# A four-layer fp32 transformer block on one core: gating of the first chunk a step earlier, normalising in halves, maxima searched one slot sooner, opening statistics spread

## The reference, cut to what matters

```python
x = x + attention_a(layernorm(x))   # 16 heads of 8, q and k RMS-normed per head, softmax, projection
x = x + feed_forward(layernorm(x))
x = x + attention_b(layernorm(x))   # differential attention: rope, 16 score heads of 8, 8 value heads of 16
x = x + feed_forward(layernorm(x))

def feed_forward(xt):               # the same weights both times
    scores = softmax(xt @ gate_w.T)             # 8 experts
    top_scores, sel = top_k(scores, 2)
    for e in range(8):                          # routed input is xt times the expert's score
        h = silu(xe @ w1[e]) * (xe @ w3[e]);  out += h @ w2[e]
    out += (silu(xt @ w1s) * (xt @ w3s)) @ w2s  # shared expert
```

## Time and profile before

| | |
|---|---|
| median of 3 runs | 957.07 us (956.77 to 957.42) |
| the profiled execution's own time | 963.01 us |
| its span, first to last instruction | 961.2 us |
| PE busy | 846.6 us (88%) |
| DVE busy | 708.4 us (74%) |
| ACT busy | 557.1 us (58%) |
| POOL busy | 575.8 us (60%) |
| mean granted clock of TensorE | 0.934 |

### The profile page before, as it was taken

How to read it: one execution, slowest core, us unless ns; L and a number is a source line. 1 busy time by engine, 2 the same in 40 slices (tenths; PEclk the granted TensorE clock), 3 DMA queues, 4 the chain that set the end, 5 groups by cost and what they waited for, 6 DMA issues and landing times.

```text
span 961.2 us, 21825 instructions
## 1 busy us (share of the span) xinstructions
PE 846.6 (88%) x6976; PEld 596.9 (62%) x6976; DVE 708.4 (74%) x1916; ACT 557.1 (58%) x888; POOL 575.8 (60%) x666
## 2 busy tenths in 40 slices
PE   3789999988988988899788888888888899898998
PEld 2455555555777777787555555555544587777786
DVE  7777777784677776776668898989865587677674
ACT  1578788875533333344378888888864444444343
POOL 4766666681666556665427676767632776566662
PEclk9999999997899999999689999999975799999999
DMA  7000000000222222221000000000000223333331
GB/s 204 17 2 1 0 0 0 1 2 15 83 80 89 89 78 77 77 89 34 1 2 3 2 1 1 1 1 1 2 2 3 88 89 100 89 100 93 94 101 44
DMA packets 35695, 42.25 MB, mean 44 GB/s; under 512 B 5936, under 2 KB 18992, under 8 KB 35632
## 3 DMA queue, kind: packets, MB, share of 16 engines
q1 hardware_dynamic: 34048, 40.85, 13.7%
q10 hardware_dynamic: 1584, 0.62, 0.2%
HBM read 38.83 MB, written 2.36 MB: 43 GB/s over the span
## 4 chain that ended last, share of the span: by engine, by line
PE 32%; POOL 25%; DVE 19%; issue 18%; DMA 3%; ACT 2%; POOLq 0%; DVEq 0%; ACTq 0%
POOL f_xe_lo L1457 8%; POOL f_p L1469 7%; DVE s_mxs L1135 6%; PE psum L392 5%; PE psum L855 3%; POOL s_inv L1089 3%; PE psum L1372 3%; PE psum L823 3%; PE psum L362 3%; PE psum L423 2%; DVE s_qt L703 2%; DMA f_gt<-gates 2%; DVE f_xe L1493 2%; PE psum L1334 2%; PE psum L378 2%
## 5 line engine op out<-in xcount | busy, mean ns | idle before, releaser
L1457 POOL TENSOR_TENSOR f_xe_lo<-f_xe,f_xe_hi 128x512 fp32r<-128x512 f32 x96 | 123.2, 1289 | 146.0 <-ACT f_xe_hi L1431 146.0
L1431 ACT ACTIVATE f_xe_hi<-f_xe 128x512 fp32r<-128x512 f32 x128 | 80.8, 631 | 222.3 <-DVE f_xe L1493 222.3
L1135 DVE TENSOR_REDUCE s_mxs<-psum 128x4 fp32r<-128x1024 f32 x128 | 155.8, 1219 | 32.4 <-PE psum L840 31.1
L1509 DVE TENSOR_TENSOR f_h<-psum,f_g 128x512 f32<-128x512 f32 x144 | 99.1, 688 | 100.4 <-PE psum L1336 55.2
L1372 PEld LDWEIGHTS psum<-w,f_h 128*128 128x128 f32 x1152 | 152.4, 197 | 17.4 <-DVE f_h L1509 7.7
L1372 PE MATMUL psum<-w,f_h 128*128 128x128 f32 x1152 | 159.4, 283 | 2.6 <-DVE f_h L1509 2.5
L996 ACT ACTIVATE s_probs<-psum 128x1024 f32<-128x1024 f32 x128 | 131.2, 1025 | 45.0 <-PE psum L823 43.1
L493 ACT ACTIVATE s_probs<-psum 128x1024 f32<-128x1024 f32 x128 | 126.2, 1023 | 32.8 <-PE psum L378 32.3
L1334 PE MATMUL psum<-f_xe_hi,w_hi 128*128 128x512 f32 x288 | 132.2, 459 | 8.6 <-POOL f_xe_lo L1457 8.6
L1335 PE MATMUL psum<-f_xe_hi,w_lo 128*128 128x512 f32 x288 | 118.1, 410 | 0.0
L1336 PE MATMUL psum<-f_xe_lo,w_hi 128*128 128x512 f32 x288 | 116.1, 403 | 0.0
(11 more groups left out here) (178 smaller groups left out, 1568.0 us busy)
## 6 DMA issues: line engine op xcount, KB each, us to landing
f_gt<-gates SPq DMA_DIRECT2D x128, 256.0 KB, 3.3
x<-in_x SPq DMA_DIRECT2D x8, 256.0 KB, 6.0
out<-x SPq DMA_DIRECT2D x8, 256.0 KB, 4.7
w<-in_w SPq DMA_DIRECT2D x3, 512.0 KB, 5.8
s_qt<-s_mt SPq DMA_DIRECT2D x32, 8.0 KB
rope_cos<-in_rope_cos SPq DMA_DIRECT2D x1, 256.0 KB, 3.3
rope_sin<-in_rope_sin SPq DMA_DIRECT2D x1, 256.0 KB, 3.1
gates<-f_sg SPq DMA_DIRECT2D x16, 16.0 KB
```

The lines of the kernel that those rows point to most:

```text
L1135: dve.tensor_reduce(mxs[:, km % 2, p, r:r + 2, :, c:c + 1].bitcast(F32R), room(km, i).rearrange("p (r j s) -> p r j s", r=2, j=2), AX.X, A ...
L1457: pool.tensor_tensor(xe_lo[:, ring(e), :], src, xe_hi[:, ring(e), :], ALU.subtract).then_inc(xe_lo_pool.sem, 1)
```

## The change

1. `STATISTICS`/`ROOTS`: parts 2 to 7 of the opening's statistics move from steps -1, 0 and 1 to one part at position 12 of each of the steps 0 to 5, their roots to position 14. `normalise` of attention a waits by a new table `NORMED`.
2. The attention steps written out singly in a go up to 5 (`PEELED_A` = 6), so the loop has three turns of two steps; in b it stays (`PEELED_B` = 2).
3. `LEAD`: positions e = 0 to 4 of the feed-forward's step -1 move from step 15 into step 14 of both attentions, e = 5 to 7 are placed at h = 7, 10, 13 of step 15.
4. `FF`: `normalise` is split into tiles 0, 1 at e = 3 and tiles 2, 3 at e = 4; `best` goes from e = 7 to 6, `index` from 8 to 7, `residual` from 3 to 4, `moments` from 6 to 7, and the root of f's statistics from e = 8 to e = 1 of the next step.
5. On PE, `x_turn` is issued after `down(e)` instead of before it.

```diff
-STATISTICS = {(-3, 0): (0,), (-3, 12): (1,), (-1, 8): (2,), (-1, 12): (3,), (0, 4): (4,), (0, 11): (5,), (1, 4): (6,), (1, 9): (7,)}
-ROOTS = {(-3, 0): (0,), (-2, 5): (1,), (-1, 13): (2, 3), (0, 14): (4, 5), (1, 14): (6, 7)}
+STATISTICS = {(-3, 0): (0,), (-3, 12): (1,), (0, 12): (2,), (1, 12): (3,), (2, 12): (4,), (3, 12): (5,), (4, 12): (6,), (5, 12): (7,)}
+ROOTS = {(-3, 0): (0,), (-2, 5): (1,), (0, 14): (2,), (1, 14): (3,), (2, 14): (4,), (3, 14): (5,), (4, 14): (6,), (5, 14): (7,)}
+NORMED = {0: 1, 2: 2, 4: 3, 6: 4, 8: 5, 9: len(PARTS)}
+PEELED_A, PEELED_B = 6, 2
...
-LEAD = {0: (0,), 2: (1,), 3: (2,), 5: (3,), 6: (4,), 12: (5,), 13: (6,), 15: (7,)}
+LEAD = {(NSEQ - 2, 5): (0,), (NSEQ - 2, 7): (1,), (NSEQ - 2, 9): (2,), (NSEQ - 2, 11): (3,), (NSEQ - 2, 13): (4,),
+        (NSEQ - 1, 7): (5,), (NSEQ - 1, 10): (6,), (NSEQ - 1, 13): (7,)}
...
 FF = {
-    "norm": 4, "x_turn": 5, "xt_sb": 5, "logits": 6, "best": 7, "pow": 7, "index": 8, "masks": 0, "sums": 1, "gates": 2,
-    "residual": 3, "stats": 5, "moments": 6, "rstd": 8, "shared": 4,
+    "norm": (3, 4), "x_turn": 5, "xt_sb": 5, "logits": 6, "best": 6, "pow": 7, "index": 7, "masks": 0, "sums": 1, "gates": 2,
+    "residual": 4, "stats": 5, "moments": 7, "rstd": 1, "shared": 4,
 }
...
-                for m, km in turned(n, k, e, "x_turn"):
-                    x_turn(m, km)
                 for m, km in turned(n, k, e, "logits"):
                     logits(m, km)
                 if run:
                     down(e)
+                for m, km in turned(n, k, e, "x_turn"):
+                    x_turn(m, km)
...
-                if first and 0 <= k - 1 < NCH and e == FF["rstd"]:
+                if first and 0 <= k - 2 < NCH and e == FF["rstd"]:
+                    pool.wait_ge(vare_sb.sem, vare_sb.upto(n - 2))
+                    pool.tensor_tensor(
+                        rstd_next[:, :].rearrange("p (n c) -> p n c", c=4)[:, (n - 2).at, :], g.f_vare[:],
+                        g.minus_half[:, 0:4], ALU.pow).then_inc(rstd_sb.sem, 1)
+
+                if first and k == NCH and e == E:
                     pool.wait_ge(vare_sb.sem, vare_sb.upto(n - 1))
...
-                if k + 2 < NCH and e == FF["norm"]:
-                    normalise(n + 2)
+                if k + 2 < NCH and e in FF["norm"]:
+                    normalise(n + 2, (0, 1) if e == FF["norm"][0] else (2, 3))
...
-    with eng.Fori(0, 5) as i:
-        body(Step(i, 2, 2), 2)
-        body(Step(i, 2, 3), 3)
-    for n in range(12, NSEQ - 1):
+    with eng.Fori(0, (12 - peeled) // 2) as i:
+        body(Step(i, 2, peeled), peeled)
+        body(Step(i, 2, peeled + 1), peeled + 1)
+    for n in range(12, NSEQ - 2):
         body(Step(None, 0, n), n)
-    for h in range(HEADS):
-        body(Step(None, 0, NSEQ - 1), NSEQ - 1, (h,))
-        for e in LEAD.get(h, ()):
-            following(Step(None, 0, -1), -1, (e,))
+    for n in range(NSEQ - 2, NSEQ):
+        for h in range(HEADS):
+            body(Step(None, 0, n), n, (h,))
+            for e in LEAD.get((n, h), ()):
+                following(Step(None, 0, -1), -1, (e,))
```

More of the change, by code:

```diff
@@ L582, in normalise @@
             def normalise(m, km):
-                if km in (0, 2, 4, 6):
-                    dve.wait_ge(g.normed, {0: 1, 2: 2, 4: 3, 6: len(PARTS)}[km])
+                if km in NORMED:
+                    dve.wait_ge(g.normed, NORMED[km])
                 dve.wait_ge(xt_mm.sem, xt_mm.upto(m - 2))
@@ L1509, in hidden, with normalise @@
                 dve.tensor_tensor(g.f_h[:, q, :], H3[q], g.f_g[:, q, :], ALU.mult).then_inc(h_sb.sem, 1)
-            def normalise(m):
+            def normalise(m, half=range(4)):
                 if k == -1:
@@ L1519, in normalise @@
                 dve.wait_ge(xt_mm.sem, xt_mm.upto(m - 1))
-                for c in range(4):
+                for c in half:
                     dve.tensor_scalar(
@@ L1662, in feed_forward, with attention_steps @@
     return layer
-def attention_steps(eng, body, first, following, tail, opening=None, preceding=None):
-    for n in range(first, 2):
+def attention_steps(eng, body, first, peeled, following, tail, opening=None, preceding=None):
+    for n in range(first, peeled):
         for h in range(HEADS):
@@ L1708, in all_steps @@
 def all_steps(eng, o, a, f, b, h):
-    attention_steps(eng, a, -3, f, TAIL_A, o)
+    attention_steps(eng, a, -3, PEELED_A, f, TAIL_A, o)
     feed_forward_steps(eng, f, b)
-    attention_steps(eng, b, -1, h, TAIL_B, None, f)
+    attention_steps(eng, b, -1, PEELED_B, h, TAIL_B, None, f)
     feed_forward_steps(eng, h)
```

## The result

The changed kernel took 936.79 us (median of 4 runs, 934.12 to 938.77), the kernel before, on the same chip, 957.25 (956.77 to 959.90). The ratio is 0.9769, 95% interval 0.9742 to 0.9797: 2.3% faster. The forecast was 921.6, the range 905 to 938. The sign was right and the time is at the slow edge of the range: 20.5 won instead of 35.5. The profiled execution took 938.77 (span 936.9), 24.3 less in span than the profiled one of before.

A forecast was written before the change was run, and what follows sets the result against it. PE, busy 88%, was held in the feed-forwards by waits and low clock. Feed-forward 23.3 + opening 4.4 + leads 5.5 and 3.0 − root 0.7 = 35.5, taken off the median 957.07: 921.6, range 905 to 938.

The forecast's parts named there:

- Rivals 1: Feed-forward: PE's new wait for `xt_sb` before `logits` drops the clock, 1.3 a step; time 934; chance 0.17.
- 2: Feed-forward: PE is the bound, the halves of `normalise` hide entirely; periods 22.4, time 902; chance 0.13.
- 4: Feed-forward: `best` is late, `pow` starts no sooner, `low(4)` stays late; f gains 1.2 a step, time 934; chance 0.05.
- the ring: Feed-forward: the cycle `hidden`, `scale`, `high`, `silu`, next `hidden`; 2.47 to 2.60, above PE's 2.30, so the next bound.
- Rival 5: Feed-forward: halves of `normalise` beside `low` delay `hidden`, 3.6 a step; time 965, chance 0.03; just cancels (957), chance 0.02.
- the 1.5 that was to count against the prediction: Feed-forward: the prediction is wrong if the two halves of `normalise` take over 1.5 each.
- 1.9 (the same wait) + 1.0 on DVE + 1.6 of low clock: Attention a, step 14: costs added to 11.9 and 1.4 of PE work (`x_turn`, `logits`), giving 17.8.
- 11.9 + 1.5 for the second chunk's gating = 13.4: Attention a, step 15: its new time; with step 14 together 31.2 against 36.7, gain 5.5.
- the 7 added to step 14: Attention b: the lead puts 7 on in step 14 and takes 7 off in step 15.
- The 3 off at the end: End of b: `pow` goes ahead of the last attention's POOL work, the 2.46 wait may go; gain 3.0.
- Rival 3: Leads give nothing: gating chain as long in step 14, stalled twice; a 0, b −3, time 933; chance 0.17.
- the length of a root: From f to b: the last chunks' root moves nearer to b's first use; 0 to −2, taken as −0.7.

The follow-up runs named there:

- e9_wlo_after_xn: The changed kernel with POOL's second `w_lo` made to wait until `normalise` of chunk 0 is through: 931.77 us, ratio 0.9708 to the kernel before.

## Why the prediction was right, and where it was off

- **Feed-forward: right in mechanism and size.** Periods 24.46 and 23.95 against 24.6 and 24.0. `pow` moved up by POOL's idle time, `low(4)` came on time in f, and the low clock went with the wait at `x_turn`. The new wait for `f_xt` is 0.9 (1.1 was forecast) and did not bring the clock down. Rivals 1, 2 and 4 fell. That the ring is now the bound rests on `hidden` waiting for `silu` and on the distance of 2.58 above PE's 2.30; PE is itself busy for 116.15 of the 122.29, so it is at most 1.2 a period below the ring, and no run moved the ring alone.
- **Rival 5** (the halves held up by `low` at every instruction) did not come in the feed-forward: 2.1 for all four, one instruction of them caught. The second half's 1.55 is just over the 1.5 that was to count against the prediction, but the first took 0.59, and the sign asked for both.
- **Opening: right**, 4.2 measured by itself (interval 1.7 to 6.9) against 4.4; both waits for `s_qt` went.
- **The step that failed is part 3, the lead of a, first in "1.9 (the same wait) + 1.0 on DVE + 1.6 of low clock".** Step 14 took 21.1 instead of 17.8. The wait was 4.33, because I went by the wait of the old place and did not look at what POOL does beside the new one: the 2.61 of `w_lo`. `e9_wlo_after_xn` shows this cause. The second term failed too: "11.9 + 1.5 for the second chunk's gating = 13.4" for step 15 was 17.5, at a clock of 0.81. Together they turned +5.5 into −1.9.
- **That the mended variant comes out at the forecast's 31.2 is luck.** Without the collision step 14 took 15.9, 1.9 under its term, since no low clock came, and step 15 took 15.2 at full clock, 1.8 over its term; the two misses cancel. With the same edit the other trace gave 33.19. What keeps step 15 above 13.4 was not tried. In both traces it opens with a wait of PE of 1.73 for `s_qt`, for which the sum had no term.
- **The lead of b was also wrong in sign**, +3.0 against −3.3. Of its terms, the 7 added to step 14 was right in size (19.1 became 25.7). The 7 taken off step 15 was 3.3: PE was 94% busy there, at a clock of 0.50 throughout. The 3 off at the end did not come: the wait of 2.46 for `hidden` is still 2.45. PE's new wait of 2.99 at `x_turn` is for a `normalise` of 1.95 that stands behind DVE's searches of maxima; that the searches are the cause was argued from the timeline, not tried.
- **Rival 3** ("the leads give nothing", 933, chance 0.17) came nearest in kind, for a reason other than the one given in a: the chain of gating was not the new stall there, one instruction on another engine was. By its number alone the 934 of rivals 1 and 4 lay as near, and neither happened.
- **Slips in the sum.** Rival 4's own terms (f gains 1.2 a step, the rest as forecast) give some 28 and 929, not 23 and 934. The 0.7 taken off as "the length of a root" stands beside a root of 1.01. Neither moves the forecast by as much as the leads did.
- **Luck.** The time lies 1.2 inside the slow edge of the range. The median missed by 15.2, nearly all of it in the leads, and the range held because it was wide enough for bad ones: the lead of a came out at its own lower bound (−2) and that of b near its (−4).

By the rule of the Trainium skill, "SBUF — State Buffer", section "SBUF: two separate sides" (one of the two engines holds the shared port pair for the whole instruction and the other fully blocks), the trace agrees, now with its full price: an instruction of 0.34 took 2.65 beside one of 2.61. In the prediction I had weighed this rule only where `low` runs, 1.3 long, and found it mild. The rule belongs wherever the moved work lands.

## What to carry to other kernels

Before work is moved, read the timelines of the *other* engines at the place where it will land, and look for the longest single instruction there, not for the average load: POOL did nothing at all for the rest of that step, and its one instruction of 2.6 cost 3 to 8 with the low clock behind it. When an experiment shows nothing, look in its trace whether the edit moved anything: a later place in a queue that is otherwise empty is the same place. Measure the parts of a change alone; here the lead lost (6.8) more than the opening had won (4.2). And when a mended variant hits the forecast, compare it term by term: a sum can be right with both of its terms wrong.

## What the runs showed of the hardware

- A `TENSOR_SCALAR` on DVE of 128x128 fp32 from on-chip memory (SBUF) to SBUF, usually 0.34, took 2.65 when POOL was in a 128x1152 `TENSOR_TENSOR` of 2.61, 1.30 beside a `low` of 1.29 in f, and 0.75 at most when `w_lo` was moved away (POOL's addition of 0.73 beside it). So the delay follows the length of POOL's instruction; it is not a share of bandwidth.
- Not every instruction of POOL does this: in the changed kernel's f, `scale` (SBUF times SBUF) at 269.22 and 271.81 took 0.68 while POOL was in `pow` (6.78 for four); in the kernel before, at 339.93 beside `low`, it took 1.76. Why `pow` differs is not shown.
- After waits of PE of 0.9 and 1.27 the matmuls behind came at full rate. After waits of about 2.0 they did either. In f of the kernel before, all six waits of 1.97 to 2.28 were followed by the half rate; in its h, of five waits of 1.98 to 2.07 only two were (below, a stretch behind such a wait that kept the clock and one that lost it); the 2.02 in step 14 of a, in the variant with `w_lo` behind, was followed by the full rate. So the length of the wait alone does not say whether the clock falls.

```profile
803.94:806.73 2.79, 2.79 (x19) 2.52 (x20) 1.15 (x2) 1.61 (x3) 0.90 (x1) 1.00 0.67 203
...
904.66:909.04 4.38, 4.38 (x19) 3.90 (x20) 1.15 (x2) 1.72 (x3) 1.28 (x1) 0.61 0.77 189
```
